# The first five turns of a software pipeline, written out by hand on five engines of Trainium2

## The reference, cut to what matters

```python
def reference(x, txt, ...):                      # x: 32 images of 3 x 224 x 224
    # tokens of an image: two convolution paths, mixed, then three more layers
    loc = dwconv(gelu(conv(x, pl_w, pl_b, stride=16)), pl_dw, pl_pw, pl_pwb)   # layer L
    g = gelu(conv(wavelet_packet(x), pg_w1, pg_b1))
    g = gelu(dwconv(g, pg_dw, pg_pw, pg_pwb))                                  # layer G
    glob = conv(g, pg_w2, pg_b2)                                               # layer W2
    h = (1.0 - gate) * loc + gate * glob
    h = relu(dwconv(h, f1_dw, f1_pw, f1_pwb))                                  # layer F1
    h = relu(dwconv(h, f2_dw, f2_pw, f2_pwb))                                  # layer F2
    h = dwconv(loc + h, f3_dw, f3_pw, f3_pwb)                                  # layer F3
    h = concat([cls, layernorm(h, ln_g, ln_b), txt])                           # 325 tokens of 192
    # attention: scores within a band of 64, no softmax; two-layer MLPs make q, k and v
    h = h + layernorm(banded(q(u), k(u)) @ v(u)),   u = layernorm(h)
    # feed-forward with activations rounded to 8 bits and ternary weights
    return h + bitlinear(silu(gate) * up, w_out),   up, gate = bitlinear(layernorm(h), w_in)
```

## Time and profile before

| | |
|---|---|
| median of 3 runs | 1143.92 us (1141.91 to 1146.18) |
| the profiled execution | 1147.13 us, its span 1145.3 us |
| PE matmul busy | 1059.6 us (93%) |
| DVE busy | 976.4 us (85%) |
| ACT busy | 881.8 us (77%) |
| POOL busy | 792.1 us (69%) |
| mean granted clock of PE | 0.971 of full speed |

### The profile page before, as it was taken

How to read it: one execution, slowest core, us unless ns; L and a number is a source line. 1 busy time by engine, 2 the same in 40 slices (tenths; PEclk the granted TensorE clock), 3 DMA queues, 4 the chain that set the end, 5 groups by cost and what they waited for, 6 DMA issues and landing times.

```text
span 1145.3 us, 19061 instructions
## 1 busy us (share of the span) xinstructions
PE 1059.6 (93%) x5641; PEld 700.3 (61%) x5691; DVE 976.4 (85%) x2829; ACT 881.8 (77%) x2173; POOL 792.1 (69%) x916
## 2 busy tenths in 40 slices
PE   6887999999999999999999999999999989888865
PEld 4554667666757575766666675757676666454522
DVE  0678868999989898999999998989899999666786
ACT  3446758697979888898979798988889787738545
POOL 4245475878787787878787778877787887646334
PEclk9888999999999999999999999999999999979988
DMA  8111010101001010101010100101010000000000
GB/s 342 43 50 40 4 50 4 50 5 58 13 22 49 11 59 10 60 11 60 7 61 5 33 38 19 51 10 60 11 60 10 18 9 12 8 16 16 16 16 22
DMA packets 23687, 41.14 MB, mean 36 GB/s; under 512 B 3649, under 2 KB 20385, under 8 KB 21281
## 3 DMA queue, kind: packets, MB, share of 16 engines
q1 hardware_dynamic: 23584, 39.93, 10.3%
HBM read 31.02 MB, written 7.99 MB: 34 GB/s over the span
## 4 chain that ended last, share of the span: by engine, by line
PE 53%; ACT 22%; DVE 16%; issue 4%; POOL 3%; DMA 2%; SPq 1%; DVEq 0%; POOLq 0%; ACTq 0%
PE bank L558 10%; PE bank L590 4%; ACT xh L1265 4%; PE bank L592 3%; PE bank L601 3%; PE bank L652 3%; ACT y_sb L1274 3%; DVE bank L1953 3%; PE bank L600 3%; ACT early L1251 2%; PE bank L776 2%; PE bank L536 2%; PE bank L708 2%; PE bank L537 2%; PE bank L654 2%
## 5 line engine op out<-in xcount | busy, mean ns | idle before, releaser
L1953 DVE SCALAR_TENSOR_TENSOR bank<-padA,c_col,bank 128x406 f32<-128x406 f32 x560 | 358.5, 640 | 9.1
L558 PE MATMUL bank<-x_sb,w_emb 128*128 128x392 f32 x576 | 221.1, 513 | 6.1 <-ACT padA L1201 3.1
L1251 ACT ACTIVATE prod<-padB,c_col 128x196 f32<-128x196 f32 x432 | 175.4, 451 | 4.9 <-DVE padB L1965 3.9
L558 PEld LDWEIGHTS bank<-x_sb,w_emb 128*128 128x128 f32 x576 | 102.0, 194 | 64.1 <-issue 12.6
L3045 POOL TENSOR_TENSOR yg<-y_f,c_gout 128x512 f32<-128x512 f32 (+2 forms) x73 | 92.9, 1273 | 52.5 <-DVE y_f L2234 52.2
L1251 ACT ACTIVATE early<-padB,c_col 128x196 f32<-128x196 f32 x288 | 118.9, 449 | 3.7 <-POOL accB L3079 3.6
L536 PE MATMUL bank<-accA,w_sq 128*128 128x196 f32 x256 | 66.5, 341 | 11.8 <-POOL accB L3079 6.8
L2214 DVE SCALAR_TENSOR_TENSOR ya<-th,bank 128x512 f32<-128x512 f32 (+2 forms) x73 | 49.9, 684 | 28.7 <-ACT th L1323 27.4
L708 PE MATMUL bank<-w_in,xq 128*128 128x512 bf16 (+2 forms) x252 | 67.1, 382 | 5.1 <-ACT xq L1317 2.4
L590 PE MATMUL bank<-xT,w_sq 128*128 128x325 f32 x192 | 64.4, 447 | 4.0 <-ACT hq L1209 3.9
L3064 POOL TENSOR_TENSOR prod<-prod 128x392 f32<-128x392 f32 x48 | 48.9, 1018 | 27.8 <-ACT prod L1251 27.7
(11 more groups left out here) (320 smaller groups left out, 3015.7 us busy)
## 6 DMA issues: line engine op xcount, KB each, us to landing
x_sb<-xt SPq DMA_DIRECT2D x16, 1176.0 KB, 5.2
out<-o_sb SPq DMA_DIRECT2D x64, 96.0 KB, 1.9
w_sq<-squares SPq DMA_DIRECT2D x1, 3840.0 KB, 15.9
h_sb<-txt SPq DMA_DIRECT2D x32, 51.8 KB
out<-o_sb SPq DMA_DIRECT2D x32, 48.0 KB, 1.9
h_sb<-txt SPq DMA_DIRECT2D x32, 44.2 KB
w_in<-win SPq DMA_DIRECT2D x1, 1024.0 KB, 17.8
h<-h SPq DMA_DIRECT2D x16, 48.0 KB, 1.9
```

The source lines that it names most:

```text
L558: done = mm(pE[:, 0:2 * N_PATCH], w_emb[:, k, m, :], x_sb[:, k, :], start=k == 0, stop=k == KC - 1)
L1251: made = go(grid(prod[ACC[s] ^ 1][:, k, :]), tap_view(padB[min(s, 2)], SIDE, k), ACT.Copy, scale=tapcol(s, 1, k))
L1953: v.scalar_tensor_tensor(grid(acc if k == TAPS - 1 else run), tap_view(pad, ROWS_A, k), tapcol(s, 0, k), grid(run), ALU.mult, ALU.add).the ...
```

## The change

`all_turns` gets a start, and each engine gets a function `fill()`, a list written out in place of turns 0 to 4. For SP, DVE, ACT and POOL it holds the same steps, in another order; the steady turn from 5 on is untouched, and so is the drain of those four. On PE the drain changes too: the wait for the last embedding goes from after `ffn_out(11, 3)` to after `transposes(13, 0)`, six `keep_busy` matmuls are put between there and `layer_F3(14)`, and further on five are taken away and two added.

```diff
-        def all_turns(turn, stop):
-            for it in range(stop):
+        def all_turns(turn, start, stop):
+            for it in range(start, stop):
                 turn(it, it % 2, [0 <= it - k < PAIRS for k in range(DEPTH)])
...
+            def fill():
+                load_x(1)
+                load_x(2)
+                load_x(3)
+                load_cls(0)
+                load_txt(0)
+                load_x(4)
+                load_txt(1)
+                load_cls(1)
...
             sp.wait_ge(s_zero, N_ZERO)
-            all_turns(turn, 17)
+            fill()
+            all_turns(turn, 5, 17)
             drain()
...
+            def fill():
...
+                layer_G(0)
+                weight_totals()
+                embed_chunk(1, EMB_BB, range(0, 2))
+                embed_chunk(1, EMB_BB, range(2, 4))
+                embed_chunk(1, EMB_BB, range(4, 6))
+                layer_W2(0)
+                embed_chunk(1, EMB_GA, range(0, 2))
+                embed_chunk(1, EMB_GA, range(2, 4))
+                layer_L(0)
+                embed_chunk(1, EMB_GA, range(4, 6))
+                embed_chunk(1, EMB_LA, range(0, 2))
+                embed_chunk(1, EMB_LA, range(2, 4))
+                embed_chunk(1, EMB_LA, range(4, 6))
+                query_key_weights()
+                embed_chunk(2, EMB_BB, range(0, 2))
+                embed_chunk(2, EMB_BB, range(2, 4))
+                layer_F1(0)
...
+                layer_L(1)
+                embed_chunk(2, EMB_LA, range(4, 6))
+                layer_F3(0)
+                embed_chunk(3, EMB_BB, range(0, 2))
+                layer_F1(1)
+                embed_chunk(3, EMB_BB, range(2, 4))
+                layer_G(2)
+                embed_chunk(3, EMB_BB, range(4, 6))
+                layer_W2(2)
+                embed_chunk(3, EMB_GA, range(0, 2))
+                embed_chunk(3, EMB_GA, range(2, 4))
+                transposes(0, 0)
+                transposes(0, 1)
+                transposes(0, 2)
+                mlp_wide(0, 'qw1', U_Q1, xT)
+                mlp_half(0, 'qw1', U_Q1, xT)
+                mlp_wide(0, 'kw1', U_K1, xT)
+                layer_F2(1)
+                embed_chunk(3, EMB_GA, range(4, 6))
...
+                mlp_half(0, 'kw2', U_K2, hk)
+                layer_F3(1)
+
             def drain():
...
                 transposes(13, 0)
+                pe.wait_ge(emb_out, PAIRS * EMBS)
+                keep_busy(1)
                 transposes(13, 1)
+                keep_busy(2)
                 transposes(13, 2)
+                keep_busy(1)
                 layer_F2(14)
                 rounded_hidden_transposes(11, 1)
                 mlp_wide(13, 'qw1', U_Q1, xT)
+                keep_busy(1)
...
                 ffn_out(11, 3)
-                pe.wait_ge(emb_out, PAIRS * EMBS)
...
+            def fill():
+                embed_out(0, EMB_BB)
+                products(0, G_, range(0, 1))
+                products(0, G_, range(1, 2))
+                products(0, G_, range(2, 3))
+                products(0, G_, range(3, 4))
+                embed_out(0, EMB_GA)
+                products(0, G_, range(4, 5))
...
+                products(0, L_, range(7, 8))
+                embed_out(0, EMB_LA)
+                products(0, L_, range(8, 9))
+                weight_sums()
+                glob_out(0)
...
+            def fill():
...
+                taps(0, L_, 5)
+                ternary_weights()
+                taps(0, L_, 6)
+                taps(0, L_, 7)
+                taps(0, L_, 8)
+                mix(0)
...
+                taps(0, F1_, 7)
+                query_key_blocks()
+                taps(0, F1_, 8)
...
+                taps(1, F2_, 2)
+                input_bn(0, range(0, 3))
+                input_bn(0, range(3, 6))
+                input_stats(0)
+                taps(1, F2_, 3)
```

More of the change, by code:

```diff
@@ L3026, in _ @@
             assert gsteps[0] == GATE_STEPS
-            all_turns(turn, 16)
+            fill()
+            all_turns(turn, 5, 16)
             drain()
```

434 lines of the change are left out of this document (428 added, 6 removed).

## The result

The changed kernel takes 1158.31 us in the median (1156.1 to 1159.78, 4 runs), the kernel before 1142.91 (1141.54 to 1146.18, 4 runs) beside it: a ratio of 1.0133, with a 95% interval of 1.0107 to 1.016. That is 15 us slower, outside the range of 1135 to 1152, on the side to which the prediction had given 0.21. The profiled execution took 1159.78 us with a span of 1158.0, against 1147.13 and 1145.3.

What follows compares the result with a forecast made beforehand. PE has no slack in steady turns, so turn 5's start counts. Fill terms gave 0.5 us later, less 0 to 0.8 in the drain: no change, 1147.5 us profiled, 1144.5 on the median's scale; range 1135 to 1152.

Steps and rivals of the forecast that it cites:

- Step 6: MLP of pair 0 and rest of turn 4: 0.4 us earlier; first MLP matmul at 131.9, turn 5 at 156.0.
- Step 7: Turn 5: 0.5 us later, as DVE's late taps delay layer F2(2), which had 0.2 us of slack on PE.
- Steps 1 and 2: Start of the fill 2.7 us later; then layer L(0) 12 us earlier, with mix(0) at 53.
- step 2: Layer L(0): 12 us earlier, with the embedding of pair 1 taking 4.2 us at full clock.
- Step 3: Weight multiplication takes most back: part two 4.5 us at full clock, F1(0) ends at 71.5, DVE 2.0 us earlier.
- Step 4: Up to the tokens of pair 0: 2.5 us earlier, F3(0) at full clock, token_add(0) ending at 114.2.
- Step 5: Text tokens, now loaded behind the class token: 2 us later, loads taking 5.7 us, input_bn(0) released at 120.4.
- rival B: Slower: waits put PE at half clock in pair 1's embedding and the weight multiplication; 7 us, 1151 us; chance 0.22.
- Step 8: Drain: keep_busy matmuls added in PE's waits gain 0; those taken off or added give 0 to 0.8 us less.
- Rival A: Faster: text loads no wall and PE bounds, turn 5 could begin 7 us earlier; 1137 us; chance 0.24.
- Rival C: The steady turn evens out an earlier or later turn 5; again 1144; chance 0.54 together with the forecast.

Runs made afterwards that it cites:

- e7: Kernel before with only the query/key weight multiplication moved from ahead of layer L(0) to ahead of layer F1(0): 1142.56 us against 1143.74, ratio 1.0000.
- k1: New compute-engine lists to about 110 us, old order behind; old load order, changed kernel's drain: 1142.25 us against 1144.2 for the kernel before, ratio 0.9981.
- e3: Kernel before with only SP's loads of turns 0 to 4 in the new order: 1155.27 us, ratio 1.0089 to before.
- e1: Changed kernel with only SP's loads of turns 0 to 4 put back in the old order: 1152.16 us against 1144.14 for the kernel before, ratio 1.0065.
- e8: e1 with layer L(1) on PE put back ahead of two embedding chunks of pair 2: 1151.15 us, ratio 1.0067 to the kernel before.
- k2: Old compute-engine lists to about 110 us, the changed kernel's behind, old load order: 1151.88 us, ratio 1.006 to the kernel before.
- e6: e1 with two embedding chunks of pair 3 moved on PE into the waits around pair 0's third transposes: 1150.3 us, ratio 1.0043 to the kernel before.
- k3: e1 with the PE edits of both e6 and e8: 1144.77 us, ratio 1.0018 to the kernel before.
- e4: Changed kernel with only pair 0's text load put back ahead of x(3): 1152.18 us, ratio 1.007 to the kernel before.
- e2: Kernel before with only the changed kernel's edits of PE's drain: 1142.54 us against 1144.14, ratio 0.9992.

## Why the prediction was wrong

The forecast was no change, 1144.5 us; it was 1158.3. (Two slips in the sum are small beside that: steps 6 and 7 as written add to 0.1 us later and not 0.5, and 1147.5 less 3.2 is 1144.3.) By its steps:

*Steps 1 and 2* held in the main. DVE's taps of L(0) began 2.3 us later (35.51 against 33.20, predicted 2.7), and `mix(0)` came at 55.1 in this execution and at 52 to 55 in others (predicted 53). PE waited 3.43 us for the weight sums, and then the embedding of pair 1 had a granted clock of 0.60 (window 40 to 46 above): its twelve matmuls took 6.9 us, where step 2 had 4.2. Step 3 had allowed 1.0 us for that.

*Step 3* was too favourable: DVE done with F1(0) at 74.1, predicted 71.5, before 73.5. Part two of the multiplication took 6.3 us, taken as 4.5: full clock for the eight wide matmuls (2.15 us), then half clock inside the matmuls of one column, at 68.46 in the rows above. The other 0.8 is that part two began at 65.13 and not at 64.3. The direction holds: e7 shows that moving the multiplication is worth nothing, and k1 that the whole first half costs nothing that can be told.

*Step 4* had F3(0) at full clock, 2.4 us for 4.8, and that is so (103.68 to 106.4, 2.7 us). But its sentence "from here to `mix(1)` DVE has no gap" was false. L(1) stands on PE behind chunks that wait 2.01 us for `embed_out` on ACT and then run partly at half clock (4.28 us for eight matmuls that take 2.80 at full, granted clock 0.66), so `mix(1)` waited 2.06 us. The tokens were done at 119.4, not at 114.2; 2.6 of the 5.2 us come from step 3 and 2.1 from this wait. I had listed L(1)'s new place only for what it covers, and not for what it waits behind.

*Step 5* failed by size. The mechanism, DVE released by the text loads, was right. The price was 6.2 us from token to `input_bn(0)` with 5.7 for the loads, and it measured 8.7 with 8.1. I had taken 159.6 us as the end of pair 1's loads, issued from 153.93, because the earlier trace rows still showed 22 GB/s up to 160. The next windows of the kernel before show that the traffic went on to 162, 8 us after the first issue:

```profile
160.00:161.00 1.00, 1.00 (x6) 0.64 (x7) 0.52 (x2) 1.00 (x3) 0.92 (x2) 1.00 0.07 22
161.00:162.00 1.00, 1.00 (x5) 0.51 (x5) 1.00 (x4) 1.00 (x4) 1.00 (x2) 1.00 0.02 7
162.00:163.00 1.00, 1.00 (x8) 0.87 (x7) 0.96 (x3) 1.00 (x4) 1.00 (x2) 1.00 0.00 0
```

With the tokens 5.2 us later than I thought and the loads 2.5 us longer, 120.4 became 128.15. On its own this list costs 11 us (e3), and taking it out of the changed kernel gives 6 (e1).

*Step 6* failed by the clock. From `input_bn(0)` to the first MLP matmul 11.1 us were needed (predicted 11.5). From there to turn 5 it was 24.1 by the sum and 27.9 by the trace: 3.8 too little. The same lists at full clock (e8, k2) need 25.0, so 2.9 of the 3.8 are the half clock in this execution (3.6 in e1), and the order itself was priced 0.9 too low. I had put the clock into rival B alone and given this stretch none of it, though waits of 3.54 us ahead of the first transposes and 2.11 ahead of the third now stand there, with nothing of the embedding between them. Whether such waits bring the clock down differs between executions (last section), so a term with both values belonged here.

*Step 7*, 0.5 us for turn 5, measured 6.6. Of that 2.0 are what the step describes, DVE late at F2(2) with 0.2 us of slack (57.5 in e1, e6, e8, k2 and k3 against 55.5), four times its size; the price had no row, only "some 0.5 us net, after the `input_bn(1)` split gives part of it back", and of the 2.0 nothing is seen to come back. Of the other 4.6 (62.1 against 57.5), 3.2 go with the loads of pair 1, by e4. The last 1.4 is the clock and not a load: e4 has the same wait for the class token (2.74 us) and the same wait of PE (2.86), and yet its PE is at 0.79 over the 8 us from 180.9 on, where the changed kernel is at 0.57 over 188 to 196 (timeline of PE in e4, for 188.84 above):

```profile
181.76 0.66 PE L547 MATMUL bank<-accA,w_sq 128*128 128x196 f32 x2 [2.86 <-issue]
```

The step never mentioned that `load_txt(1)` and `load_cls(1)` move too, from 154 us to behind x(4), where SP's issues take until 182.7 and DVE waits 2.85 us for the class token.

*Step 8* held: e2, 0.9992 (0.9976 to 1.0009).

The sum therefore missed 5.2 us up to the tokens, 2.5 at the loads, 3.8 at the MLP, 0.4 from there to x(4) and 6.1 in turn 5, and counted 0.4 too much in step 6. That is 17.6 us at x(5), of which the shorter drain of the profiled execution gives back 5. Rival B named one of the causes, for the most part in the wrong place. It put the clock into the embedding of pair 1 and the weight multiplication, priced it at 7 us, and would decide when part two took over 7 us; the embedding did run slow, but part two took 6.3, and the clock fell at the MLP of pair 0 and at 188.8 all the same. Rival A, that turn 5 starts earlier with the text loads no wall, falls with e3. Rival C, that the steady turn absorbs a shift, falls in every row of the table: x(6) less x(5) is 62.3 throughout.

## What to carry to other kernels

A load that is moved behind a step on the path has to be priced from its first issue to the moment its reader starts, in a run of the reader, and every load that the list moves needs its own line in the sum, the second pair's too. A large idle number behind a reordered step is no measure of its cost (11 us of DVE for nothing): first ask what the step would wait for in its old place. Where short steps of one chain stand on PE in one block, enter the waits between them once alone and once with half clock over what follows, and let the range hold both.
